# Second attention of a two-layer block: bias adds on TensorE, fewer ScalarE sums, last heads in two halves

## The reference

```python
# layer 0: distance attention, and seven experts with one shared one
d2 = max(q2[:, None] + k2[None, :] - 2 q k, 1e-12)
att0 = (softmax(-sqrt(d2)) @ v) @ wo.T + bo
ffn0 = 0.5 / w * shared(x) + switched(x) / w
# layer 1: the second attention
att = softmax(einsum('blhd,bmhd->blmh', q, k) * scale, axis=2)
att1 = einsum('blmh,blhd->blhd', att, v) @ w_out.T + b_out
ffn1 = sqrt((x @ cos(theta + tn))**2 + (x @ sin(phi + pn))**2)
```

## Time and profile before

| | |
|---|---|
| three timed runs | 1525.82, 1529.29, 1529.65 us, median 1529.29 |
| the profiled execution | 1526.65 us, span 1524.9 us, 21409 instructions |
| mean granted TensorE clock | 0.927 |
| busy: ACT, DVE, PE, POOL | 95%, 83%, 74%, 29% of the span |
| second attention: first exp, last exp ends | 1020.8 us, 1513.7 us |
| exps of the second attention | 428 plain, 84 with the sum on ACT |

### The profile page before, as it was taken

One profiled execution on the slowest core, in us unless ns is written; L12 is line 12 of the kernel. 1 busy time (PEld: TensorE's weight loads), 2 busy tenths in 40 slices (PEclk: granted clock), 3 DMA queues, 4 the chain that ended last, 5 costly groups with the idle time before them and its releaser, 6 DMA issues.

```text
span 1524.9 us, 21409 instructions
## 1 busy us (share of the span) xinstructions
PE 1130.1 (74%) x7876; PEld 441.3 (29%) x7876; DVE 1259.5 (83%) x2254; ACT 1450.4 (95%) x798; POOL 437.3 (29%) x314
## 2 busy tenths in 40 slices
PE   4587786877778878878888765776677677675765
PEld 2133223142332433424425311232132122221212
DVE  6987978959589899898897777857898898897886
ACT  3799999979799999999999999999999999999997
POOL 5284450652603123033022230043123124122100
PEclk8598988988999999999999997899999999999999
DMA  4842644212152121121121321043033133031001
GB/s 119 241 125 62 172 124 120 59 49 67 53 156 63 41 56 50 41 67 50 42 52 41 87 72 34 20 122 67 27 109 82 26 109 82 26 104 31 26 26 56
DMA packets 104034, 112.71 MB, mean 74 GB/s; under 512 B 41698, under 2 KB 76002, under 8 KB 103922
## 3 DMA queue, kind: packets, MB, share of 16 engines
q1 hardware_dynamic: 98202, 98.63, 23.9%
q0 software_dynamic: 4464, 11.09, 2.6%
q10 hardware_dynamic: 1256, 1.53, 0.4%
HBM read 66.52 MB, written 44.70 MB: 73 GB/s over the span
## 4 chain that ended last, share of the span: by engine, by line
ACT 63%; DVE 14%; PE 12%; issue 9%; another core or an unknown queue 1%; DMA 1%; ACTq 0%; DVEq 0%; SPq 0%
ACT scores L628 22%; ACT scores L617 21%; ACT exp L1144 14%; DVE scores L592 7%; DVE exp L1151 4%; PE pvb L573 3%; ACT exp L1140 3%; PE ring L1120 2%; PE ring L558 2%; PE ring L839 2%; ACT L628 1%; ACT ht L878 1%; ACT L617 1%; PE ring L850 1%
## 5 line engine op out<-in xcount | busy, mean ns | idle before, releaser
L592 DVE TENSOR_SCALAR scores<-ring 128x1024 f32<-128x1024 f32 x512 | 589.3, 1217 | 24.4 <-PE ring L558 24.3
L628 ACT ACTIVATE scores<-scores 128x8192 f32<-128x8192 f32 x64 | 445.8, 7021 | 0.2
L1144 ACT ACTIVATE exp<-ring 128x1024 f32<-128x1024 f32 x428 | 414.9, 1272 | 9.4 <-PE ring L1120 9.4
L617 ACT ACTIVATE scores<-scores 128x8192 f32<-128x8192 f32 x60 | 417.2, 7021 | 0.7 <-DVE scores L592 0.6
L1120 PE MATMUL ring<-stk 128*128 128x512 bf16 x1024 | 310.4, 387 | 135.2 <-ACT exp L1144 105.8
L573 PE MATMUL pvb<-scores,val 128*9 128x256 f32 x4096 | 324.0, 392 | 83.5 <-issue 38.7
L1151 DVE SCALAR_TENSOR_TENSOR exp<-exp 128x512 f32<-128x512 f32 x428 | 332.1, 799 | 62.9 <-ACT exp L1144 57.3
L558 PE MATMUL ring<-stk 64*128 64x512 bf16 x1024 | 210.0, 407 | 62.8 <-DVE scores L592 45.3
L1120 PEld LDWEIGHTS ring<-stk 128*128 128x128 bf16 x1024 | 62.5, 98 | 357.2 <-ACT exp L1144 264.0
L558 PEld LDWEIGHTS ring<-stk 64*128 64x128 bf16 x1024 | 49.9, 93 | 294.5 <-DVE scores L592 203.4
L613 POOL DMA_DIRECT2D att<-attg x32 | 25.2, 790 | 371.9 <-DVE attg L606 371.1
(11 more groups left out here) (241 smaller groups left out, 1176.5 us busy)
## 6 DMA issues: line engine op xcount, KB each, us to landing
stk<-stack SPq DMA_DIRECT2D x190, 192.0 KB, 2.9
stack<-qp SPq DMA_DIRECT2D x7, 768.0 KB, 4.8
stack<-kp SPq DMA_DIRECT2D x7, 768.0 KB, 3.9
xj<-xg SPq DMA_DIRECT2D x10, 448.0 KB, 4.3
yg<-yj POOLq DMA_DIRECT2D x10, 448.0 KB, 3.6
stack<-qp SPq DMA_DIRECT2D x7, 512.0 KB, 5.1
stack<-kp SPq DMA_DIRECT2D x7, 512.0 KB, 4.9
stk<-sum_rows SPq DMA_DIRECT2D x126, 24.0 KB
```

Source lines behind the costliest of these rows:

```text
L592: nc.vector.tensor_scalar(S[place][:, j * N:(j + 1) * N], tile, 1e-12, None, ALU.max).then_inc(o.release(("qk", group, place, j)), 1)
L617: nc.scalar.activation(S[place][:], S[place][:], ACT.Sqrt).then_inc(root_done, 1)
L628: nc.scalar.activation(S[place][:], S[place][:], ACT.Exp, scale=-1.0).then_inc(exp_done, 1)
L1144: nc.scalar.activation(EX[i // 2][:, i % 2, :], tile, ACT.Exp, scale=SCALE1).then_inc(o.release(("qk1", n, i)), 1)
```

## The change

Four things.

1. `sum_by_act` takes every fifth tile: 16, 21, ..., 121, 22 a batch for 28.
2. `add_bias` sends, ahead of a projection's own matmuls and into the same PSUM tile, the identity times the broadcast bias row: one fp32 matmul of 512 columns for four token blocks. The projection then accumulates onto it. POOL's `pool_base` and `pool_bias` go, with their semaphores; DVE's add waits for the load of `X` instead.
3. In the last batch, tiles 96 to 127 (the last four heads) run in another order: four token blocks of each of the four heads, then the other four of each (`tile_at`).
4. So the first half of the tokens is weighed after tile 111, turned at tiles 116 and 117, projected at 121 to 123 and added after tile 124, in `aux`; only the second half is left after the last tile.

```diff
@@ -73,7 +73,19 @@
 
 def sum_by_act(n, i):
     s = n % H * NT + i
-    return n < HEADS - H and 12 <= s < 124 and s % 4 == 1
+    return n < HEADS - H and 12 <= s < 124 and s % 5 == 1
+
+
+
+
+LAST_GROUP = (H - GROUP) * NT
+
+
+def tile_at(b, s):
+    if b < B - 1 or s < LAST_GROUP:
+        return b * H + s // NT, s % NT
+    half, left = divmod(s - LAST_GROUP, GROUP * NT // 2)
+    return HEADS - GROUP + left // (NT // 2), half * NT // 2 + left % (NT // 2)
 
 
 FOLDS = [0]
...
 
-        def pool_base(pool, b):
-            pool.wait_ge(late_in, 48)
-            pool.wait_ge(X_in, 16 * (b + 1))
-            nc.gpsimd.tensor_tensor(X[b][:, :, :], X[b][:, :, :], bcast(late["bo0"], 1, NT), ALU.add).then_inc(based, 1)
-
...
 
+        def add_bias(tile, name, tokens=NT):
+
+            for t in range(0, tokens, 4):
+                nc.tensor.matmul(tile[:, t * P:(t + 4) * P].rearrange("p (t c) -> p t c", c=D), ident,
+                                 bcast(late[name], 1, 4), start=True, stop=False)
+
         def pe_project_att(pe, o, b, slot):
             tile = o.begin(pe, ("awo", b), slot)
             pe.wait_ge(late_in, 48)
+            add_bias(tile, "bo0")
             o.emptied(pe, ("aturn", b))
             for t in range(NT):
                 mm = nc.tensor.matmul(tile[:, t * P:(t + 1) * P], att_t[:, t * P:(t + 1) * P], late["wo0"],
-                                      start=True, stop=True)
+                                      start=False, stop=(t % 4 == 3))
                 if t % 2 == 1 and t < NT - 1:
                     yield
             mm.then_inc(ring_full, 1)
...
@@ -968,7 +982,7 @@
 
         def dve_add_att(dve, o, b):
             tile = o.filled(dve, ("awo", b))
-            dve.wait_ge(based, b + 1)
+            dve.wait_ge(X_in, 16 * (b + 1))
             nc.vector.tensor_tensor(X[b][:, :, :], X[b][:, :, :], tile.rearrange("p (t c) -> p t c", c=D), ALU.add
                                     ).then_inc(o.release(("awo", b)), 1)
 
...
-
-        def pool_bias(pool, b):
-            pool.wait_ge(xn1_ready, NT * (b + 1))
-            nc.gpsimd.tensor_tensor(X[b][:, :, :], X[b][:, :, :], bcast(late["bo1"], 1, NT), ALU.add).then_inc(biased, 1)
 
...
-        def act_exp1(act, o, n, i):
+        def act_exp1(act, o, b, s):
+            (n, i), k = tile_at(b, s), s % NT
             tile = o.filled(act, ("qk1", n, i))
             if n:
-                if i % 2 == 0:
-                    act.wait_ge(summed, FOLDS[NT * (n - 1) + i + 2])
+                if k % 2 == 0:
+                    act.wait_ge(summed, FOLDS[b * H * NT + s - NT + 2])
             elif i == 0:
...
 
+        def dve_weigh_last(dve, half):
+            u, b, rows = GROUPS - 1, B - 1, slice(half * NT // 2, (half + 1) * NT // 2)
+            part, sums_of = wsum[u % 2][:, :, rows], den[u % 2][:, :, rows]
+            dve.wait_ge(summed, FOLDS[b * H * NT + LAST_GROUP + (half + 1) * GROUP * NT // 2])
+            nc.vector.reciprocal(part, sums_of).then_inc(inv_done, 1)
+            dve.wait_ge(inv_done, u + 1 + half)
+            nc.vector.tensor_tensor(part, part, sums_of, ALU.mult).then_inc(w_done, 1)
+            dve.wait_ge(w_done, u + 1 + half)
+            vals = V1[b][:, rows, u % PER_BATCH * 32:(u % PER_BATCH + 1) * 32].rearrange("p t (h e) -> p t h e", e=HD)
+            for h in range(GROUP):
+                mul = nc.vector.tensor_tensor(vals[:, :, h, :], vals[:, :, h, :], bcast(part[:, h, :], 2, HD), ALU.mult)
+            mul.then_inc(weighed, 1)
+
 
 
         def pe_turn_end(pe, o, b, slot):
...
 
         def pe_project_end(pe, o, b, slot):
             tile = o.begin(pe, ("fwo", b), slot)
+            add_bias(tile, "bo1")
             o.emptied(pe, ("fturn", b))
             for t in range(NT):
                 mm = nc.tensor.matmul(tile[:, t * P:(t + 1) * P], fatt[:, t * P:(t + 1) * P], late["wo1"],
-                                      start=True, stop=True)
...
             tile = o.begin(pe, ("fturn", B - 1, half), slot)
-            if half == 0:
-                pe.wait_ge(weighed, PER_BATCH * B)
+            pe.wait_ge(weighed, PER_BATCH * B + half)
             for t in range(4):
                 mm = nc.tensor.transpose(tile[:, t * P:(t + 1) * P], V1[B - 1][:, 4 * half + t, :], ident)
+                if t == 1:
+                    yield
             mm.then_inc(ring_full, 1)
+            yield
 
         def dve_keep_last(dve, o, half):
             tile = o.filled(dve, ("fturn", B - 1, half))
             nc.vector.tensor_copy(fatt[:, HALVES[half]], tile[:, 0:512]).then_inc(o.release(("fturn", B - 1, half)), 1)
 
-        def pe_project_last(pe, o, half):
-            tile = o.begin(pe, ("fwo", B - 1, half))
+        def pe_project_last(pe, o, half, slot):
+            tile = o.begin(pe, ("fwo", B - 1, half), slot)
+            add_bias(tile, "bo1", 4)
+            yield
             o.emptied(pe, ("fturn", B - 1, half))
             for t in range(4):
                 mm = nc.tensor.matmul(tile[:, t * P:(t + 1) * P], fatt[:, (4 * half + t) * P:(4 * half + t + 1) * P],
-                                      late["wo1"], start=True, stop=True)
+                                      late["wo1"], start=False, stop=(t % 4 == 3))
+                if t % 2 and t < 3:
+                    yield
             mm.then_inc(ring_full, 1)
+            yield
 
         def dve_add_last(dve, o, half):
             tile = o.filled(dve, ("fwo", B - 1, half))
...
+        WEIGH_HALF_AT = LAST_GROUP + GROUP * NT // 2
+        TURN_HALF_AT, WO_HALF_AT = WEIGH_HALF_AT + 4, WEIGH_HALF_AT + 9
...
-                for half in range(2):
-                    pe_turn_last(pe, o, half, None)
-                for half in range(2):
-                    pe_project_last(pe, o, half)
+                        if b == B - 1:
+                            if s == TURN_HALF_AT:
+                                turn_last = pe_turn_last(pe, o, 0, AUX)
+                            if s in (TURN_HALF_AT, TURN_HALF_AT + 1):
+                                next(turn_last)
+                            if s == WO_HALF_AT:
+                                project_last = pe_project_last(pe, o, 0, AUX)
+                            if WO_HALF_AT <= s < WO_HALF_AT + 3:
+                                next(project_last)
+                at_once(pe_turn_last(pe, o, 1, None))
+                at_once(pe_project_last(pe, o, 1, None))
 
...
-                for n in range(HEADS):
+                for n in range(HEADS - GROUP):
...
-                        if i == NT - 1 and n % GROUP == GROUP - 1:
+                        if i == NT - 1 and n % GROUP == GROUP - 1 and n < HEADS - 1:
                             dve_weigh(dve, n // GROUP, summed, FOLDS[NT * (n + 1)])
-                dve.wait_ge(mag_added, B)
-                for half in range(2):
-                    dve_keep_last(dve, o, half)
-                for half in range(2):
-                    dve_add_last(dve, o, half)
+                        if b == B - 1:
+                            if s == WEIGH_HALF_AT - 1:
+                                dve_weigh_last(dve, 0)
+                            if s == TURN_HALF_AT + 1:
+                                dve_keep_last(dve, o, 0)
+                            if s == WO_HALF_AT + 3:
+                                dve.wait_ge(mag_added, B)
+                                dve_add_last(dve, o, 0)
+                dve_weigh_last(dve, 1)
+                dve_keep_last(dve, o, 1)
+                dve_add_last(dve, o, 1)
 
             by_guard(dve, general, fast)
```

More of the change, by code:

```diff
@@ L1139, in act_exp1 @@
                     act.wait_ge(w_done, n // GROUP - 1)
-                nc.scalar.activation(EX[i // 2][:, i % 2, :], tile, ACT.Exp, scale=SCALE1,
+                nc.scalar.activation(EX[k // 2][:, k % 2, :], tile, ACT.Exp, scale=SCALE1,
                                      accum_out=den[n // GROUP % 2][:, n % GROUP, i:i + 1]
@@ L1143, in act_exp1, with dve_fold @@
             else:
-                nc.scalar.activation(EX[i // 2][:, i % 2, :], tile, ACT.Exp, scale=SCALE1
+                nc.scalar.activation(EX[k // 2][:, k % 2, :], tile, ACT.Exp, scale=SCALE1
                                      ).then_inc(o.release(("qk1", n, i)), 1)
-        def dve_fold(dve, o, n, i):
+        def dve_fold(dve, o, b, s):
+            (n, i), k = tile_at(b, s), s % NT
             o.emptied(dve, ("qk1", n, i))
             if not sum_by_act(n, i):
-                tile = EX[i // 2]
+                tile = EX[k // 2]
                 nc.vector.scalar_tensor_tensor(
-                    out=tile[:, i % 2, 0:N // 2], in0=tile[:, i % 2, 0:N // 2], scalar=1.0,
-                    in1=tile[:, i % 2, N // 2:N], op0=ALU.mult, op1=ALU.add,
+                    out=tile[:, k % 2, 0:N // 2], in0=tile[:, k % 2, 0:N // 2], scalar=1.0,
+                    in1=tile[:, k % 2, N // 2:N], op0=ALU.mult, op1=ALU.add,
```

(10 more changed lines are left out.)

28 lines of the change are left out of this document (10 added, 18 removed).

## The result

The changed kernel takes 1539.6 us (median, 1537.69 to 1540.54). The kernel before, run beside it, takes 1529.4 us: ratio 1.0069, interval 1.0057 to 1.0082. So it is slower, by 10.2 us of median, where 8.2 were forecast. The profiled execution took 1539.14 us, with a span of 1537.4 us for 1524.9.

A forecast was written before the change was run, and what follows sets the result against it. ACT was taken to bound the kernel, at 0.917 us per tile in the second attention; terms -1.5, +2.1, +8.8, +0.2 and -1.4 sum to +8.2 us, which on the median 1529.3 gives 1537.5 us, range 1530 to 1543.

The forecast's parts named there:

- 18 sums fewer on ACT: Three batches of the second attention: 22 sums for 28 on ACT, 0.081 us each, -1.5 us.
- one more fold before the V copy: Before the mix at tile 108: one more DVE fold delays V copy and exp, three times, +2.1 us.
- bias matmuls in the loop: Projection jobs in the loop: 1.72 us of bias matmuls on PE pause ACT 1.46 us six times, +8.8 us.
- tile 122: Last batch: the bias matmul at tile 121, 0.86 us alone, opens a job and pauses ACT, +0.2 us.
- tail: From last fold to the end: half the work left, 4.6 us for 5.8 and 0.25 less weighing, -1.4 us.
- Round 13: Batch 0's projection: bias matmuls end within 0.2 us of DVE's copy that PE awaits; zero, otherwise 1.7 us.
- POOL's adds: Two POOL adds per batch go: DVE gets 2.1 us back twice a batch, none on ACT's path; zero.
- then eight records, 2.04: End of the kernel: the last projection's eight PE records after the bias matmul take 2.04 us at half clock.
- Rival D: End of the kernel: bias matmul replaces the second half, so the tail keeps its length; 1.4 us, no chance given.
- A: Loop projections: bias matmuls nearly free or count not binding, pauses near 0.5 us six times, +2.3 us, 1531.6; chance 0.14.
- B: Loop: DVE holds ACT and POOL held DVE, so mix pauses go; -7.4 us, 1522; chance 0.06.
- C: At the mix or a bias step: PE falls to half clock on top, +3.4 to +6 us, 1541 to 1543.5; chance 0.15.

The follow-up runs named there:

- g2: g1 with fills of the aux buffer counted by a semaphore of their own; ratio 0.9954 to the kernel before.
- e3: The kernel before with only the new rule for the sums, every fifth tile on ACT; ratio 1.0011 to the kernel before.
- f3: The change with every bias matmul of the whole projections sent twice; ratio 1.0129 to the kernel before.
- f2: The change with fills of the aux buffer counted by a semaphore of their own; ratio 1.0008 to the kernel before.
- e2: The kernel before with only the bias adds moved to PE; ratio 1.0075 to the kernel before.
- h1: The change with PE biases spread over four tiles where aux is free, aux fills counted apart, first mix step at tile 109; ratio 0.9954 to the kernel before.
- f1: The change with each projection's bias matmuls spread over the four tiles ahead, end projection at tile 38; ratio 1.0069 to the kernel before.
- f5: f1 with the end turn moved to tile 31 and the projections to 22 and 43, clear of aux; ratio 1.0012 to the kernel before.
- e1: The change with its bias adds given back to POOL; ratio 1.0017 to the kernel before.
- e4: The kernel before with only the last four heads in halves, biases on POOL; ratio 0.9986 to the kernel before.
- f4: e4 with both mix steps two tiles later, at 109 and 119; ratio 0.9970 to the kernel before.
- g1: e1 with only the first mix step two tiles later, at 109; ratio 0.9960 to the kernel before.

## Why the prediction was right, and where it was not

The direction and the mechanism held; the measured 1539.6 us are 2.1 us above the forecast of 1537.5 and inside the range. No step of the path to the six pauses failed; the tail was mis-sized, the pause at tile 12 was left out, and a part of the growth forecast for tile 108 came at tile 98. By the steps, in the second attention:

| term | forecast | measured |
|---|---|---|
| 18 sums fewer on ACT | -1.5 | -1.5 |
| one more fold before the V copy | +2.1 | +2.0 |
| bias matmuls in the loop | +8.8 | +8.7 |
| tile 122 | +0.2 | +0.3 |
| tail | -1.4 | -2.0 |
| not foreseen: tile 12 twice, tile 11 | 0 | +0.3 |
| sum | +8.2 | +7.9 |

*The sums.* 0.081 us each by the pace: the -1.5 is 18 x 0.081 again, and not a measurement of its own. g2's full batches (119.1 us) bear it out. *The fold.* The forecast put the whole 0.69 us a batch on tile 108. It came as 0.47 there and 0.22 at tile 98, and e3 has the same split with no other edit. In the third batch half clock came on top (3.01 us), but the first batch had none this time (1.43 for 2.64). So the right sum is partly luck: the term is -0.99 us in the first batch, +0.69 in the second and +2.3 in the third.

*The bias matmuls.* The step-by-step timeline came out within 0.02 us in five of six pauses: two calls take 1.72 us, exp 27 starts 0.04 us behind scores 28, and the pause is 1.44 us five times and 1.52 once, for 1.46. f3 and f2 show both halves of the reasoning, the one-for-one growth and the count. The Trainium skill ("TensorE: Matmul & The Clock Gate", section "Step-by-step: what each phase is for") gives a time of purely the number of columns; here an fp32 matmul of 512 columns is two records of 0.43 us at granted clock 1.00, 0.86 us in all, four times the 0.21 us estimated from that page, and the measurement decides.

*Round 13.* Nothing, as forecast: in e2 the bias matmuls end 0.18 us behind DVE's copy, and from ACT's first exp behind them (857.31 us in e2, 856.9 in e3, which has no bias on PE) to the first exp of the second attention both take 144.1 us. The change takes 144.7, the 0.5 at 931 us above among them; f2 and h1, which have those matmuls too, take 144.1 to 144.2.

*POOL's adds.* DVE did get time back, 3.4 us a batch in e2 and 2.9 in h1 against g2, where the forecast had twice 2.1, in the direction of the rule in the Trainium skill ("SBUF — State Buffer", section "Who interferes with whom"); no time came of it, as the 0.96 us at tile 108 of e2 show.

*The tail* came out at -2.0 us for -1.4. The step that was off is "then eight records, 2.04", at half clock. In the change they took 1.33 us in the chain, since PE's clock was back at 2.4 GHz at 1533.54. That belongs to this one execution and not to the kernel. f1, f2, f3, f5 and h1 end with the same code, and in all five the clock stays at 0.50 over PE's work in the tail. The chain of h1:

```profile
1507.87 1.71 PE ring L971 x2
1509.58 1.72 PE ring L1259 x8
```

Their tails are 9.76 to 9.80 us, and 10.29 in f5, where the end of DVE's add stands as in the others and the rest, behind it, is longer. That is 1.5 us under the kernel before, the forecast's size. Without a bias matmul there (e1, e4, f4, g1, g2) the tail is 9.26 to 9.28 us, at half clock too:

```profile
1499.58 2.06 PE ring L1250 x8
```

```profile
1497.60:1505.00 7.40, 3.13 (x12) 2.48 (x12) 1.38 (x2) 0.00 (x0) 0.00 (x0) 0.50 0.12 35
```

So the bias matmul costs the tail 0.5 us at half clock: of its 1.7 us, 0.86 lie where PE in e4 waits for the copy, and the projection behind it takes 1.72 us in the chain instead of 2.06. In the change the clock hid that cost. Rival D falls: with the bias in it the tail is still 1.5 us shorter than before at half clock.

*What was left out.* A pause of 0.26 and 0.29 us at tile 12, in the change, of 0.18 to 0.29 in f1, f3 and f5, and, as 0.38 at tile 13, in h1, but in neither g1 nor g2. All of these have PE biases and the new rule for the sums. But e2, with PE biases and the old rule, doesn't have it, nor e1 and e3, with the new rule and POOL's adds, nor f2, with both and a count for `aux`. No row shows what it waits for, and it stays open. Open too are the 4.6 us ahead of the second attention. The ratio makes the change 10.6 us slower and the second attention explains 7.9. In nine of the twelve experiments too the ratio lies above what the second attention has, by 1.0 us in g1 up to 5.0 in e1 and 5.8 in f1; in e4, f2 and f5 it lies 1.3 to 1.6 us under it, and those are the ones whose profiled execution had the clock fall at tile 108 in two or three batches. The forecast held this stretch at zero. Profiles are single executions and f5's twelve runs lie between 1526.8 and 1538.1 us, so it may be scatter, or an effect of the altered program on a stretch that it doesn't touch; no run told them apart.

*The rivals.* A falls with four records of 0.43 us and with the exp behind scores 28; without the count (f2), it is what happens, 0.57 us. B falls with e2. C had its half clock once, as the kernel before had, with nothing added in sum.

My own misses among the experiments: e1 was to be under before and is 2.7 us above it by the medians; e2's tail was to grow 3.3 us and grew 0.46; f1's placement ran into a buffer that I had not followed through; the pause at tile 108 in f2 was to fall and did not.

## What to carry to other kernels

Work that is added to an engine with free time costs by where it stands before it costs by how much it is: look for the shortest distance to an instruction that the bounding engine waits for, cut the work so that each piece fits into the idle time of one tile, and then check that its buffer is free at the new place. One semaphore that counts fills of several buffers makes each fill wait for those begun earlier; a count of its own for `aux` took 0.87 us off each of the six pauses here. And where a change of 8 us is made of several parts, first read the pauses of the bounding engine one by one: each part had its own tile.

## What the runs showed of the hardware

The granted clock of PE after a wait is not settled by the length of that wait alone. Ahead of the first mix matmul PE waits 0.99 us in each batch of the kernel before, e2 and e4; 1.46 us in the change, e1, e3, f1, f3 and f5; and 1.68 us in f2. Of these 30 waits 15 came with a fall of the granted clock to 0.50 (1.2 GHz): one in three in most of the kernels, two in e4, all three in f2 and in f5. In one and the same execution the change waited 1.46 us three times and fell once. In f4, g1, g2 and h1, where PE doesn't wait there, it fell in none of 12. Each fall costs ACT about 1.6 us (3.01 for 1.43).

In the tail PE is idle 4.0 to 4.3 us ahead of its work, and the clock is at 0.50 when the work begins or within 0.1 us of it, in all fourteen kernels. In the change and in e2, where it fell last, just as PE began, it was back 3.4 us after the fall; in the five other kernels with the change's tail it stayed at 0.50 until PE was done. More work in the tail is therefore not what brought it back.
